# First pass of a five-pass convolution and attention kernel: fixed slots over three images, first layer by parts, two logarithm phases an image

## The reference

```
mu = x.mean(-1); var = ((x - mu)**2).mean(-1)
x_norm = (x - mu) / sqrt(var + EPS) * gamma + beta
x_gray = x_norm.mean(-1)
grad_h, grad_v = mean |differences of x_gray along w, along h|      # one number each per image
scores = [grad_h, grad_v, 0.8*(grad_h + grad_v)*0.5, |grad_h - grad_v|]
idx = argmax(softmax(relu(scores @ sel_w1 + sel_b1) @ sel_w2 + sel_b2)) % 4
x_sel = swap rows and columns of x_norm if idx == 1 else x_norm     # per image
t = x_sel.reshape(b, h*w, c) @ fc1_w + fc1_b                        # 96 -> 192
t = depthwise convolution of 3 taps along the 3136 pixels + dw_b
out = x + gelu(t) @ fc2_w + fc2_b                                   # 192 -> 96
```

## Time and profile before

| | |
|---|---|
| median of 3 runs | 11815.99 us (11809.92 to 11818.07) |
| the profiled execution | 11807.14 us, with a span of 11805.3 us |
| the first pass, in the profile | first transpose at 70 us, last fc2 matmul at 2146.8 us |
| TensorE, mean granted clock | 0.977 of full speed |

### The profile page before, as it was taken

One profiled execution on the slowest core, in us unless ns is written; L12 is line 12 of the kernel. 1 busy time (PEld: TensorE's weight loads), 2 busy tenths in 40 slices (PEclk: granted clock), 3 DMA queues, 4 the chain that ended last, 5 costly groups with the idle time before them and its releaser, 6 DMA issues. The chain is left out here.

```text
span 11805.3 us, 397033 instructions
## 1 busy us (share of the span) xinstructions
PE 11116.6 (94%) x158740; PEld 8317.4 (70%) x158740; DVE 7378.2 (62%) x12642; ACT 7831.3 (66%) x13524; POOL 5227.8 (44%) x6916
## 2 busy tenths in 40 slices
PE   6999999899999999998989999998999999999999
PEld 2444444577777777777767777776888888788887
DVE  4444444577777777775447777776666666666665
ACT  4555555477777777776337777775777777777776
POOL 0000000377777777775014544443555555555554
PEclk9999999899999999999989999998999999999999
DMA  1111111122222222222643333332010000010100
GB/s 54 39 40 36 40 35 40 33 53 50 52 51 51 51 52 51 51 51 77 216 146 80 81 79 79 80 79 54 24 25 24 25 24 24 25 25 25 24 24 22
DMA packets 1105622, 617.63 MB, mean 52 GB/s; under 512 B 864651, under 2 KB 1076566, under 8 KB 1099704
## 3 DMA queue, kind: packets, MB, share of 16 engines
q1 hardware_dynamic: 1091496, 553.66, 19.3%
q10 hardware_dynamic: 12288, 38.54, 1.0%
HBM read 308.38 MB, written 282.75 MB: 50 GB/s over the span
## 5 line engine op out<-in xcount | busy, mean ns | idle before, releaser
L1484 POOL TENSOR_TENSOR L_HdL<-L_Hd,L_HdH 128x392 fp32r<-128x392 f32 x1536 | 1572.7, 1024 | 283.8 <-POOL L_HdH L1482 283.1
L1468 POOL TENSOR_TENSOR L_SQ<-L_X 96x392 f32<-96x392 f32 x512 | 428.5, 837 | 2298.8 <-DMA L_X<-after_L 2288.6
L991 PE MATMUL banks<-L_ident,L_PR 113*113 113x113 f32 x9216 | 1201.1, 267 | 1.2 <-DVE L_X L1390 0.7
L991 PEld LDWEIGHTS banks<-L_ident,L_PR 113*113 113x113 f32 x9216 | 1143.1, 180 | 63.8 <-DVE L_X L1390 9.8
L1219 ACT COPY L_PT<-banks 113x452 f32<-113x452 f32 x1792 | 885.8, 538 | 371.1 <-PE banks L991 369.2
L1235 ACT ACTIVATE L_PR<-L_SX 113x588 f32<-113x588 f32 x1536 | 1088.0, 708 | 52.3 <-DVE L_SX L1362 10.3
L1482 POOL CAST L_HdH<-L_Hd 128x392 fp32r<-128x392 f32 x1536 | 785.1, 511 | 740.5 <-issue 658.1
L395 PE MATMUL banks<-scan_XS,scan_W1T 97*96 (+1 forms) x2688 | 1111.4, 552 | 0.0
L1054 PE MATMUL banks<-L_VB,L_PT 113*49 113x34 f32 x36864 | 1064.1, 213 | 2.0 <-ACT L_PT L1219 1.0
L1262 ACT ACT_TABLE_LOAD x512 | 656.9, 1283 | 607.3 <-PE banks L998 607.2
L1356 DVE TENSOR_REDUCE L_MX<-banks 113x12 f32<-113x588 f32 x1024 | 783.4, 765 | 432.2 <-PE banks L1037 432.2
(11 more groups left out here) (239 smaller groups left out, 27006.6 us busy)
## 6 DMA issues: line engine op xcount, KB each, us to landing
L_X<-after_L SPq DMA_DIRECT2D x768, 147.0 KB
after_L<-L_X SPq DMA_DIRECT2D x512, 147.0 KB
conv_T<-L_norm_by_phase SPq DMA_DIRECT2D x96, 512.0 KB, 3.3
L_norm_by_phase<-L_XP SPq DMA_DIRECT2D x512, 84.0 KB, 2.1
scan_XT<-in_x SPq DMA_DIRECT2D x33, 1176.0 KB, 7.1
L_norm<-L_XA SPq DMA_DIRECT2D x256, 147.0 KB, 1.9
L_conv<-conv_D ACTq DMA_DIRECT2D x96, 392.0 KB, 3.0
L_XR<-L_norm SPq DMA_DIRECT2D x256, 147.0 KB, 2.6
```

The source lines that it names most:

```text
L991: mm = pe.transpose(bank(TURN[a])[0:SPAN, (k % 4) * SPAN:(k % 4 + 1) * SPAN], PR[:, st.v if lag else st.u, 2 * k:2 * k + 2, :].rearrange(" ...
L1484: pool.tensor_tensor(HdL[:, u, j].bitcast(F32R), Hd[:, u, j], HdH[:, u, j], ALU.subtract).then_inc(s[f"hd_parts_{j}"], 1)
```

## The change: a new schedule of the first pass

- The loop over images is written out. There are B + 3 steps; in step i the norm of image i, the selector and blend of image i-1 and the convolution of image i-2 run together. Each engine visits each slot in the same fixed order.
- `conv_half` becomes nine float32r matmuls instead of three float32 ones: W1TH with XSH, W1TH with XSL, W1TL with XSH, for each of three taps. Their weights are split once in front of the loop.
- POOL now squares (`square`) and splits the blended block into XSH and XSL (`split`: a copy and a subtraction). DVE blends into a small two-deep XS.
- ACT no longer squares. It takes the logarithms and exponentials of two groups at a time, at slots 4 and 9, in place over RS, and copies the turned blocks (`copy_turned`) instead of DVE, at slots 11 to 13.
- `fc2_block` and `residual` of a block run four slots behind its first half block (`BEHIND`). Hd has three buffers instead of two, XM three, XN two.
- In front of the loop there are two more blocks: the split of the weights, and the filling of the constant row and the edges of XSH and XSL on DVE.

```diff
+    BEHIND = 4
+    MEAN_AT, VAR_AT, LOGS_AT, NORMED_AT = {1: 0, 2: 1, 6: 2, 7: 3}, {3: 0, 4: 1, 8: 2, 9: 3}, {4: (0, 1), 9: (2, 3)}, {5: (0, 1), 10: (2, 3)}
+    TURN_AT = {11: (0, 1), 12: (2, 3), 13: (4, 5, 6)}
+    DIFFS, SUMS, SCORE, SEL1, SEL2, EXPO, FLAG = 2, 3, 5, 6, 7, 8, 9
+    BLEND_AT = {9: (0,), 10: (1, 2), 11: (3,), 12: (4,), 13: (5, 6)}
...
+        def over_slots(step):
+            for i in range(B + 3):
+                for k in range(SLOTS):
+                    unit = (i - 2) * SLOTS + k
+                    if unit < UNITS + 2 * NB:
+                        step(i, k, i < B, 1 <= i <= B, i + 1 < B, unit)
...
                     for t in range(3):
-                        mm = pe.matmul(PS[0:C, 4 + k % 3, 0:TB], W1T[0:C + 1, t, h * C:(h + 1) * C],
-                                       xs[:, m * TB + t:m * TB + t + TB], start=(t == 0), stop=(t == 2))
+                        cols = slice(m * TB + t, m * TB + t + TB)
+                        for n, (wt, xt) in enumerate(((W1TH, XSH), (W1TH, XSL), (W1TL, XSH))):
+                            mm = pe.matmul(PS[0:C, CONV_BANKS[unit % 3], 0:TB], wt[0:C + 1, t, h * C:(h + 1) * C].bitcast(F32R),
+                                           xt[:, c % 2, cols].bitcast(F32R), start=(t == 0 and n == 0), stop=(t == 2 and n == 2))
...
+                # PE, one slot
+                def step(i, k, norm, sel, turn, unit):
+                    if 0 <= unit < UNITS:
+                        conv_half(unit)
+                    if norm and k in MEAN_AT:
+                        mean(i, MEAN_AT[k])
+                    if norm and k in VAR_AT:
+                        variance(i, VAR_AT[k])
+                    if turn:
+                        for m in TURN_AT.get(k, ()):
+                            turn_block(i + 1, m)
...
+                    if due(unit) is not None:
+                        fc2_block(due(unit))
...
+                # ACT, one slot
+                    if 0 <= unit < UNITS:
+                        gelu(unit)
+                    if norm and k in LOGS_AT:
+                        act.preload_act_table_set(LOG_EXP)
+                        for g in LOGS_AT[k]:
+                            logs(i, g)
+                        for g in LOGS_AT[k]:
+                            exps(i, g)
+                    if turn:
+                        for m in TURN_AT.get(k, ()):
+                            copy_turned(i + 1, m)
...
+                # DVE
+                def blend(p, m):
+                    n = p * NB + m
+                    if n >= 2:
+                        dve.wait_ge(s["xs_parts"], n - 1)
+                    xs = XS[:, n % 2]
+                    dve.tensor_scalar(xs, XN[0:C, p % 2, m * TB:(m + 1) * TB], fb[:, 1:2], None, ALU.mult).then_inc(s["blend"], 1)
+                    dve.wait_ge(s["blend"], n + 1)
...
+            @block.gpsimd
+            def _(pool):
+                def square(i, g):
+                    pool.wait_ge(s["xm"], i * NGR + (g + 1))
...
+                def split(p, m):
...
+                    pool.wait_ge(s["xs"], n + 1)
+                    pool.tensor_copy(high.bitcast(F32R), XS[:, n % 2]).then_inc(s["xs_high"], 1)
+                    pool.wait_ge(s["xs_high"], n + 1)
+                    pool.tensor_tensor(XSL[0:C, p % 2, cols].bitcast(F32R), XS[:, n % 2], high, ALU.subtract).then_inc(s["xs_parts"], 1)
```

More of the change, by code:

```diff
@@ L269, in scan_pass @@
                                  "dve_chain", "centred", "expo", "flag", "flagb", "flag_ready", "factors", "blend", "xs",
[L270 removed]
+                                 "xs_high", "xs_parts", "conv", "gelu", "fc2", "out")}
         stored, passed = [sem("stored0"), sem("stored1")], sem("passed")
@@ L284, in group_banks, with stores_of, stored_through, due @@
             return PS[0:rows, b0:b0 + n, 0:TB]
[L286 to L298, removed]
+        def stores_of(n):
+            return 16 * (4 if n % NB == 0 else 2)
+        def stored_through(n):
+            return sum(stores_of(q) for q in range(n % 2, n + 1, 2))
+        def over_slots(step):
[4 more added lines that the diff above has]
+                        step(i, k, i < B, 1 <= i <= B, i + 1 < B, unit)
+        def due(unit):
+            n, odd = divmod(unit - BEHIND, 2)
+            return n if not odd and 0 <= n < BLOCKS else None
         with nc.Block() as block:
@@ L521, in _ @@
+                for m in range(NB):
+                    copy_turned(0, m)
+                over_slots(step)
             @block.vector
             def _(dve):
-                Xv = X[:].rearrange("c (p j) -> c j p", j=TP)
-                XNT = XN[0:C, :].rearrange("c (h w) -> c w h", w=W)
-                def copy_turned(n, m):
-                    dve.wait_ge(s["turned"], n * NB + (m + 1))
-                    if m == 0 and (not isinstance(n, int) or n >= 1):
-                        dve.wait_ge(s["mean"], n * NGR)
-                    dve.tensor_copy(Xv[:, 4 * m:4 * m + 4, :], PS[0:C, m % 4, 0:TB].rearrange("c (j p) -> c j p", j=4)).then_inc(s["x_ready"], 1)
@@ L628, in step @@
-                    if conv:
-                        residual(c, old, NB - 1)
-                for m in range(NB):
-                    copy_turned(0, m)
-                over_images(dve, step)
+                    if norm and k in MEAN_AT:
+                        centred(i, MEAN_AT[k])
+                    if norm and k in NORMED_AT:
+                        for g in NORMED_AT[k]:
+                            normed(i, g)
+                    if sel and k == DIFFS:
+                        dve.wait_ge(s["grey_tiles"], i * 32)
+                        dve.tensor_tensor(DH[:, 0:W - 1], GH[:, 1:W], GH[:, 0:W - 1], ALU.subtract).then_inc(s["diffs"], 1)
+                        dve.tensor_tensor(DV[0:H - 1, :], GN[0:H - 1, :], GH[0:H - 1, :], ALU.subtract).then_inc(s["diffs"], 1)
@@ new lines, in step @@
+                    if sel and k == FLAG:
+                        dve.wait_ge(s["flagb"], i)
+                        if i >= 2:
+                            dve.wait_ge(s["xs"], (i - 1) * NB)
+                        dve.tensor_copy(fb[:], PS[0:C, SEL_BANK, 0:2]).then_inc(s["factors"], 1)
+                        dve.wait_ge(s["factors"], i)
+                    if sel:
+                        for m in BLEND_AT.get(k, ()):
+                            blend(i - 1, m)
+                    if due(unit) is not None:
+                        residual(due(unit))
```

379 lines of the change are left out of this document (165 added, 214 removed).

## The result

The kernel after takes 11434.24 us (median of 4 runs, 11430.40 to 11434.97), against 11815.3 us for the kernel before on the same chip. The ratio is 0.9677, with a 95% interval of 0.9661 to 0.9694.

A forecast was written before the change was run, and what follows sets the result against it. PE was taken to bound the first pass; a step of 52.8 us work plus 1.2 stall, 54.0 against 64.17, gave 295 over 29 steps, plus 38, less 35: 298 us gained, so 11518 us, 8-in-10 range 11440 to 11665.

The forecast's parts named there:

- The bound: First pass: TensorE (PE) bounds the step, busy 58.0 of 63 us with little idle.
- The price of a part: Scan convolution: each float32r matmul of 448 columns takes 0.205 us, so nine make 1.85 us a half.
- The first rival: Scan convolution gains nothing on PE: matmul distances of 0.23 us and full toll, step 57.5, total 11630; chance 0.13.
- the fourth: Rival: float32r matmuls whose columns start one element off take 0.375 us, kernel slower, about 12200; chance 0.05.
- the toll of 0.2 us: Scan convolution: a round trip between float32 and float32r matmuls costs 0.2 us, in 12 of 14 slots.
- The stall: Slot 12 of a step: PE waits for a late residual before fc2, 1.2 us with its restart.
- The waits that go: PE's three waits (first turn for logarithm, variance for square, fc2 for residual), 4.3 us a step, go with most lower-clock time.
- ACT and POOL were no bound: In a step ACT stays at or below 35 of 53 us and POOL is at 26 of 53.
- The second rival: DVE and POOL exclude each other fully from slot 9 on: 4.5 us a step more, 11660; chance 0.20.
- The third rival: Steps of the first pass have no toll and no stall: 50.4 us a step, 11400; chance 0.07.
- Start and end: First pass outside the 29 full steps: 38 us gained before step 2, 35 lost behind the last.
- Written out instead of looped, at nothing: Image loop as straight code: loop bodies are fetched again every pass anyway, so writing it out costs nothing.

The follow-up runs named there:

- residual first: Against the kernel after, DVE does the residual of slot 10 ahead of the two normalisations and two blends; 11419.7 us, ratio 0.9667.
- four phases: Against the kernel after, logarithms and exponentials run one group at a time, at slots 4, 5, 9 and 10; 11746.8 us, ratio 0.9940.
- one part: Against the kernel after, only the product high x high is kept, three float32r matmuls a half instead of nine; 11134.5 us, ratio 0.9425.
- copies on DVE: Against the kernel after, DVE instead of ACT copies the turned blocks, behind the slot's residual; 11583.4 us, ratio 0.9804.
- double split: Against the kernel after, POOL does each split's subtraction twice, with a semaphore passage between; 11530.8 us, ratio 0.9760.

## Why the prediction was wrong, step by step

- **The bound was read right.** PE bounds the step before and after; a convolution in float32 with the new schedule keeps PE busy for all of 1400 us.
- **The price of a part was right.** 0.205 us, from the earlier trace rows scaled by columns, is what the timeline shows. The first rival (0.23 and no gain) is out, and so is the fourth: nine matmuls with starts zero, one and two columns off take 1.85 together.
- **The failed step: the toll of 0.2 us in "a half costs 1.85 + 0.2 x 12/14 = 2.02".** Between float32 and float32r matmuls of 448 columns it is nothing. That makes 2.4 us a step (28.3 - 25.9), 70 of the 78 us that the steps gained more than forecast. The earlier trace rows did show two long distances, but I gave them to the change of type. Their float32 neighbours are small matmuls (32x98 in the row itself), and the kernel after has the extra 0.07 to 0.09 only beside one-column matmuls. The trace of before already showed that such neighbours cost time without any change of type:

```profile
230.92 0.18 PE L433 MATMUL banks<-scan_gone,scan_GA 56*4 56x1 f32 x2 [0.54 <-issue]
231.05 2.49 PE L395 MATMUL banks<-scan_XS,scan_W1T 97*96 x6
233.38 0.54 PE L407 MATMUL banks<-scan_Hd,scan_W 96*97 96x448 f32 x1
```

  A float32 half behind float32 one-column matmuls takes 233.38 - 231.05 = 2.33, against 2.26 elsewhere. No type changes there, and 0.07 is lost all the same. But small neighbours are not the whole story of L1. In that pass a border between matmuls of 392 columns is long as well, in the trace of before:

```profile
4005.70 0.34 PE L998 MATMUL banks<-L_XN2H,L_W1L 97*128 97x392 f32 x1
4005.99 0.90 PE L1072 MATMUL banks<-L_OT,L_Wp 97*97 97x392 f32 x2
4006.71 0.39 PE L998 MATMUL banks<-L_XNH,L_WkH 97*96 97x392 f32 x1
```

  From float32r to float32 it is 0.29 here instead of 0.18, and two float32 records take 0.72 instead of some 0.66. So the toll was read from real rows of L1 and fails when carried to the scan; what causes it in L1, and with it the 0.08 in the earlier trace rows, stays open.
- **The stall was mis-sized.** The residual is late once a step in slot 12, as laid out, but it costs 0.5 us with its restart (residual first) where I took 1.2. The layout had the bare delay at 0.2; the rest I had added for the exclusion and the restart. That is 0.7 us a step. Against both stands 0.4, which is by difference (50.78 of the kernel residual first, less the 50.4 of the sum without toll and stall). Most of it is the selector's four small matmuls: 265.64 to 266.33 is 0.69 where two distances of 0.205 would be 0.41, so each costs 0.28 and the four 1.1, against the 0.8 taken. 54.0 - 2.4 - 0.7 + 0.4 = 51.3, the measured step.
- **The waits that go were right**: two are gone and the residual's is down to 0.3 us. The lower clock went with them: the step of before had 1.3 us of it, the step of after none. Where an experiment put waits of over 2 us a step back, the granted clock fell as well (0.93 with four phases, 0.94 with one part, 0.96 with copies on DVE, 0.99 with the double split).
- **ACT and POOL were no bound, as said.** ACT takes 29.5 us a step (forecast: at or below 35) and POOL 19.1 (forecast 26, priced high). DVE takes 28.6 where 24 was forecast, in part the instructions that POOL's work holds up.
- **Table loads** are six a step, as counted.
- **The second rival** (0.20) was right that the engines hold one another up, and wrong about the price. The Trainium skill (SBUF — State Buffer, Who interferes with whom) says that a DVE instruction with two SBUF inputs and a POOL instruction that reads SBUF exclude each other, the first to issue holding the port for its whole length. The trace agrees that they hold one another up, and only in part that it is for the whole length: the one-column instruction ends with POOL's square, but the blend beside the split goes from 1.07 to 1.59, where standing still until the subtraction ended would make it 1.87. And the lengthened chain of DVE and POOL fits inside TensorE's 51 us: DVE waits 7.0 us for splits in 27 steps, and it took a doubled subtraction to make it 82.5.
- **The third rival** (no toll, no stall; 50.4 a step, 11400) was the nearest to what happened, and I had given it 0.07. With the stall taken away by hand the step is 50.78 and the total 11420.
- **Start and end** were off by 8 and 4 us: the start gained 46.4 for 38, the end lost 31.0 for 35. At the start the setup up to the first `mean` grew by 2.4 us (76.97 to 79.35) where 7 were forecast, and step 0 took 29.0 instead of 42.9, so 13.9 less where 7 were forecast; step 1 took 33.3 for 31. At the end steps 32 and 33 took 79.0 together where 83 were forecast.
- **Written out instead of looped, at nothing.** True of the pass itself, which shows no waits. But code that changes its length moves the loops behind it: L2 lost 29 us and L1 gained 20, each with the set of waits that came or went, and with L3 and the conv pass the later passes lost 16 us that I had not thought of. This loss hid part of the miss in the steps, by luck.

In profiled time the change gained 372.3 us, 74 more than forecast: the steps +78, start and end +12, the later passes -16.

## What to carry to other kernels

A toll read off one border has two candidate causes, the change and the neighbours; look in the same trace for the same neighbours without the change, and for the change with the neighbours of the loop at hand, before it goes into a sum fourteen times a step. When every wait of the bounding engine is closed by hand-placed slots, a full schedule laid out in time can find the right wait and still overstate its size, as here (1.2 for 0.5). Splitting the table phases of a helper engine in a schedule made for fewer cost more here (10.4 us a step) than the faster arithmetic on the bounding engine gained (5.4). A pass that isn't edited can still move by 1% when code in front of it changes length, so compare passes one by one.

## What the runs showed of the hardware that was not expected

- In the scan a float32r matmul of 448 columns follows another at 0.205 us at any column offset of 0 to 2, and follows or precedes float32 matmuls of 448 columns at no cost. In the L1 pass a border between the types at 392 columns did cost 0.11 us (0.29 for 0.18). Beside one-column matmuls 0.07 to 0.09 us are lost each time, whatever the type.
- A strided copy of 448 elements out of PSUM takes 1.06 us on ACT and 1.00 on DVE.
- POOL's square takes 1.68 us for 896 columns and 0.93 for 448. A subtraction of two different tiles of 448 columns takes 0.98 with DVE idle beside it, so reading one tile twice saves little.
- A DVE instruction on four numbers grew from 218 to 758 ns beside a POOL instruction.
- L2's length moves between 2106 and 2135 us with the position of PE's code, with 9 or 18 waits of some 3 us that the profile gives no releaser for.
